# Layer 0's gate and up products by Strassen's seven products, with the down weights' Hadamard products inside the units

## The chip, the cores and the metric

The kernel runs on one core of a Trainium2 chip. The metric is the device time of one execution in microseconds (us); shown is the median of several executions. A core has TensorE (PE: matrix products into the eight banks of PSUM), VectorE (DVE), ScalarE (ACT), GpSimd (POOL, which does not read PSUM) and SyncE (SP, which issues transfers). Each engine works its own list of instructions in order; semaphores are the only order between engines.

## The reference

Two transformer layers over 2048 tokens of width 512. The part that is changed is the feed-forward block of layer 0. Its activations are 2048 wide, and a fast Walsh-Hadamard transform stands between the product of gate and up and the down projection:

```python
def fwht(x): ...                      # orthogonal, along the last axis, n = 2048
up_gate = jnp.einsum('bsd,hd->bsh', x, W1)      # (tokens 2048, 512) x (512, 2048)
up_lin  = jnp.einsum('bsd,hd->bsh', x, W3)
hidden  = jax.nn.silu(up_gate) * up_lin
hidden  = fwht(hidden)
out     = jnp.einsum('bsh,dh->bsd', hidden, W2)  # 2048 -> 512
...
h = _layernorm(x) * (1 + cb) + sb
x = x + gb * _L0_ffn_ref(h, W1, W2, W3)
```

The transform is symmetric, so the kernel applies it to the down weights W2 instead of to the activations. Layer 1 has linear attention (`_L1_attn_ref`) and then a feed-forward block of width 1408 without the transform.

## The kernel before, in words

Precision: each f32 factor is split into a high part (a cast to fp32r) and a low part (what is left), and a product of two such factors is three matmuls into one bank: high by high, low by high, high by low. That is `product`, lines 219 to 233, so all these matmuls have the lines 227, 228 and 229 whatever they compute; the names of their operands tell them apart.

Stages of one execution: modulation vectors and the projections of layer 0 (to some 206 us), softmax attention (to 776 us), output projection with the norm behind it (to 830 us), feed-forward of layer 0 (to 1375 us), layer 1's projections with linear attention (to 1530 us), its output projection and norm (to 1611 us), and its feed-forward block (to the end).

Layer 0's block is `feed_forward` (line 445). It takes the hidden width in segments of two chunks of 128, and for each segment goes over four blocks of 512 tokens. A step (one segment, one block) has two units, one for each chunk: a gate and an up product of 4 x 3 matmuls each (`up`). The down product of a step (`down_`, 4 tiles of 2 x 3 matmuls) comes one step later on PE, and DVE adds each tile to the residual `x` (`add_x`, line 736). Per unit ACT takes the Silu of the gate bank (line 678) and casts the hidden chunk's high part (661); DVE multiplies (763) and makes the low part (725). The Hadamard transform of the down weights is in two parts. GpSimd makes the part across the 16 chunks during attention and stores it as `w2_mixed`; the part inside a chunk is a product on PE with a 128 x 128 Hadamard matrix, `mix` (lines 559 and 560, two matmuls a chunk, 16 chunks, each once). The normed tokens stand ready as high and low parts for all 2048 tokens (`h2_hi`, `h2_lo`), and GpSimd has nothing to do in this block after the first weights.

Layer 1's block is `winograd_forward` (line 792). There gate and up of one chunk for a pair of 512-token blocks are a 2 x 2 product of blocks (gate and up rows by halves of the 512 inputs, against token halves), made by seven products instead of eight. A *unit* is one chunk and one half (1024) of the tokens; all chunks of the first half come first, then all of the second. A product is 2 x 3 matmuls. The seven left factors are sums of weight blocks: GpSimd makes four sums (`weight_sums_gpsimd`, lines 954 to 959), ACT casts the high parts in four pieces (`weight_hi_scalar`, 1010) and GpSimd makes the low parts (`weight_lo_gpsimd`, 1015). The seven right factors are made once for each half of the tokens, from four token sums (lines 967 to 978; for the first half on DVE, for the second on GpSimd in units 3 to 6), ACT casts (1038) and DVE low parts (1042). What comes out of the seven products is put together by ACT (`snapshot_scalar`, line 1101, product 0) and seven additions on DVE (1165 to 1196); then come Silu (1107), the product of gate and up (1205), the high part (1120) and low part (1213), for each of the two blocks. Products go round five banks, (7u + j) % 5.

The down product follows by segments, q, of two chunks (one chunk in a few segments of layer 1, whose width has 11 chunks). While the units of segment q are computed, PE makes the 8 tiles of segment q-1: in each unit one behind product 3, two behind product 4, one behind product 5 (`place_of`, line 892). Three banks serve them in turn, and a tile waits until the tile three before it has been added. The down weights of segment q are loaded, multiplied by the gate row on GpSimd (`down_gate_gpsimd`, 985, in the segment's first unit, behind the weight work of that unit, line 999), cast on ACT (1127) and made low on DVE (`down_lo`, 1229, behind the second and third tile's additions).

The order in which each engine does this is written out by hand in `Stage.tensor`, `Stage.scalar`, `Stage.vector` and `Stage.gpsimd`, and nothing else plans it. `projection_and_norm` (line 379) leads the output projection of layer 0 into `feed_forward`; `projection_and_pairs` (line 1283) does it in layer 1, and it also makes there the right factors of the first token half (`operand_hi_scalar`, `operand_lo_vector`, `token_sum_vector`). At the end of layer 0's block `linear_projections` (line 1374) hooks in its first norm: statistics, standard deviation, transposes.

In the prediction *first unit* and *second unit* of a segment are its chunks c = 0 and c = 1.

## Time and profile before

| | |
|---|---|
| median of 3 executions | 1983.14 us (1980.57 to 1985.82) |
| the profiled execution's own time | 1980.84 us |
| its span in the trace | 1978.6 us |
| PE busy | 1897.5 us, 96% |
| DVE, ACT, POOL busy | 1170.3, 707.6, 759.0 us |
| mean granted TensorE clock | 0.991 of full speed |

The profile page gives the busy time of each engine, the span in 40 slices, and the groups of instructions that cost most. PE's busy share is the sum of overlapping matmuls' recorded times, each ending later than the next begins; so 100% says that PE never stood still, and the distance of two starts is what a matmul costs. The trace can also be asked for windows of time, for the instructions of one engine in order, and for who waited for whom.

### The profile page before, as it was taken

How to read it: one execution, taken by the hardware profiler on the slowest of the kernel's cores; microseconds unless marked ns; L12 is line 12 of the kernel's file. 1: busy time of each engine (PE TensorE's matmuls, PEld its weight loads, DVE VectorE, ACT ScalarE, POOL GpSimd, SP SyncE). 2: the span in 40 equal slices, each digit the busy share in tenths (PEclk: the TensorE clock that was granted, in tenths of full speed). 3: DMA queues.
4: the chain of work that ended last, by engine and by line, in shares of the span. 5: the costliest groups of instructions: out<-in, count | busy, mean ns of one | idle time of the engine just before them, and what ended most of it. 6: DMA issues, size and time to landing. Idle time of an engine off the chain costs nothing. (4 is left out here: it accounts for less than half of the span.)

```text
span 1978.6 us, 26382 instructions
## 1 busy us (share of the span) xinstructions
PE 1897.5 (96%) x9936; PEld 1360.3 (69%) x9936; DVE 1170.3 (59%) x1956; ACT 707.6 (36%) x1275; POOL 759.0 (38%) x722
## 2 busy tenths in 40 slices
PE   7999999999999999899999999999999889998999
PEld 5677555555545545688888888887887567787877
DVE  5466877676666742853434343444432797778776
ACT  4221355555546565421111111113321234334332
POOL 1122678788776589300000000001000615656563
PEclk9999999999999999999999999999999999999999
DMA  9753422322321203110000000002000111111211
GB/s 325 267 152 113 98 55 56 87 54 56 87 44 34 60 12 107 59 43 32 32 2 33 32 23 10 0 20 70 11 6 0 33 32 49 54 54 43 89 57 53
DMA packets 80783, 120.83 MB, mean 61 GB/s; under 512 B 7008, under 2 KB 38768, under 8 KB 80624
## 3 DMA queue, kind: packets, MB, share of 16 engines
q1 hardware_dynamic: 73200, 93.96, 16.6%
q0 software_dynamic: 7456, 25.18, 4.2%
q8 instruction: 79, 1.29, 0.3%
q14 instruction: 48, 0.39, 0.1%
HBM read 93.68 MB, written 25.44 MB: 60 GB/s over the span
## 5 line engine op out<-in xcount | busy, mean ns | idle before, releaser
L1831 DVE TENSOR_REDUCE part_max<-banks 128x1 f32<-128x512 f32 (+2 forms) x640 | 356.9, 614 | 149.1 <-PE banks L1803 90.9
L2356 ACT ACTIVATE probs<-banks 128x512 f32<-128x512 f32 (+3 forms) x640 | 311.1, 538 | 268.7 <-PE banks L2271 133.3
L1803 PE MATMUL banks<-kst,qst 96*128 96x512 f32 (+2 forms) x640 | 261.3, 417 | 12.1 <-DVE part_max L1831 9.6
L2267 PE MATMUL banks<-qst,kst 98*128 98x512 f32 (+2 forms) x640 | 251.2, 412 | 0.7 <-ACT probs L2356 0.7
L1465 POOL TENSOR_TENSOR w_lo<-early_weights,w_hi 128x512 fp32r<-128x512 f32 x4 | 5.1, 1310 | 544.1 <-ACT w_hi L1439 544.1
L763 DVE TENSOR_TENSOR tokens_b<-banks,tokens_b 128x512 f32<-128x512 f32 x64 | 44.3, 692 | 251.7 <-ACT tokens_b L678 251.7
L2217 POOL TENSOR_TENSOR early_weights<-probs 128x512 f32<-128x512 f32 (+2 forms) x152 | 160.5, 1085 | 56.6 <-ACT probs L2356 56.1
L2217 POOL TENSOR_TENSOR pairs_own<-probs 128x512 f32<-128x512 f32 (+2 forms) x152 | 157.2, 1063 | 63.7 <-ACT probs L2356 63.4
L678 ACT ACTIVATE tokens_b<-banks 128x512 f32<-128x512 f32 x64 | 38.3, 598 | 395.6 <-PE banks L229 395.6
L2267 PEld LDWEIGHTS banks<-qst,kst 98*128 98x128 f32 x640 | 123.6, 194 | 64.3 <-issue 49.0
L1803 PEld LDWEIGHTS banks<-kst,qst 96*128 96x128 f32 x640 | 123.5, 193 | 59.9 <-DVE part_max L1831 47.1
L2308 PE MATMUL banks<-probs,tokens_a 128*32 128x512 f32 (+3 forms) x1280 | 140.6, 541 | 0.6 <-DVE tokens_b L2386 0.6
L227 PE MATMUL banks<-w_b_hi,w_a_hi 128*128 128x512 f32 x308 | 123.2, 400 | 16.4 <-DVE w_b_lo L1042 7.1
L228 PE MATMUL banks<-w_b_lo,w_a_hi 128*128 128x512 f32 x308 | 120.8, 392 | 0.0
L229 PE MATMUL banks<-w_b_hi,w_a_lo 128*128 128x512 f32 x308 | 120.7, 392 | 0.0
L736 DVE TENSOR_TENSOR tokens_a<-banks,tokens_a 128x512 f32<-128x512 f32 x128 | 86.8, 688 | 46.2 <-PE banks L229 46.2
L227 PE MATMUL banks<-f_d_hi,f_hid_hi 128*128 128x512 f32 x256 | 101.4, 396 | 1.3 <-DVE tokens_a L736 1.3
L228 PE MATMUL banks<-f_d_lo,f_hid_hi 128*128 128x512 f32 x256 | 100.1, 391 | 0.0
L229 PE MATMUL banks<-f_d_hi,f_hid_lo 128*128 128x512 f32 x256 | 100.1, 391 | 0.0
L227 PE MATMUL banks<-h_hi,f_w_first 128*128 128x512 f32 x256 | 99.7, 389 | 0.0
L228 PE MATMUL banks<-h_lo,f_w_first 128*128 128x512 f32 x256 | 99.6, 389 | 0.0
L229 PE MATMUL banks<-h_hi,f_w_first 128*128 128x512 f32 x256 | 99.6, 389 | 0.0
(263 smaller groups left out, 4188.1 us busy)
## 6 DMA issues: line engine op xcount, KB each, us to landing
tokens_a<-in_L_wmod SPq DMA_DIRECT2D x12, 1024.0 KB, 7.3
qst<-q_hi SPq DMA_DIRECT2D x32, 256.0 KB, 6.1
kst<-k_hi SPq DMA_DIRECT2D x32, 256.0 KB, 8.2
tokens_b<-in_down_wt SPq DMA_DIRECT2D x10, 512.0 KB, 3.5
q_hi<-qk_out_hi POOLq DMA_DIRECT2D x16, 256.0 KB, 3.5
q_lo<-qk_out_lo POOLq DMA_DIRECT2D x16, 256.0 KB, 3.4
k_hi<-qk_out_hi POOLq DMA_DIRECT2D x16, 256.0 KB, 3.8
k_lo<-qk_out_lo POOLq DMA_DIRECT2D x16, 256.0 KB, 4.2
```

Of the source, the lines that this page charges most:

```text
L227: nc.tensor.matmul(dst, lh, rh, start=(first and i == 0), stop=False)
L228: nc.tensor.matmul(dst, lh, rl, start=False, stop=False)
L229: mm = nc.tensor.matmul(dst, ll, rh, start=False, stop=(last and i == n - 1))
L678: nc.scalar.activation(silu[:, u % 2, :], bank[2 * (u % 2)][:], ACT.Silu, scale=1.0 if mixed else gs[:, ch:ch + 1]).then_inc(silu_s, 1)
L736: nc.vector.tensor_tensor(xt, bank[4 + n % 3][:], xt, ALU.add).then_inc(x_added, 1)
L763: nc.vector.tensor_tensor(act_[:, u % 2, :], up_bank, silu[:, u % 2, :], ALU.mult).then_inc(hid_s, 1)
L1803: mm = nc.tensor.matmul(dst[:, 0:wide], qst[n % QS][0:BIASROW, h, P * t:P * t + P], kst[(NB * g + c) % KS][0:BIASROW, h, 0:wide], start=Tr ...
L1831: nc.vector.tensor_reduce(part_max[:, n % 2, ht, c:c + 1], max_bank(slot)[:, 0:wide], AX_X, ALU.max).then_inc(max_read, 1)
L2217: nc.gpsimd.tensor_tensor(pairs[o % 2][:, h, c0:512], probs[:, 2 * s % PS, h, c0:512], probs[:, (2 * s + 1) % PS, h, c0:512], ALU.add).the ...
L2267: mm = nc.tensor.matmul(dst[:, c0:512], kst[ck % KS][0:BIASROW + 2, h, at:at + P], qst[n % QS][0:BIASROW + 2, h, c0:512], start=True, stop ...
L2308: mm = nc.tensor.matmul(bank[6][HD * h:HD * h + HD, c0:512], v[:, kt, at:at + HD], probs[:, q % PS, h, c0:512], start=(kt == 0), stop=(las ...
L2356: nc.scalar.activation(probs[:, q % PS, h, c0:512], score_bank(sh)[:, c0:512], ACT.Exp, scale=SCALE).then_inc(exp_done, 1)
```

## The change

`feed_forward` and `projection_and_norm` are deleted. Layer 0's block is now made by `winograd_forward`, which takes a mode `mixed` for the case without scales and with Hadamard weights. With 16 chunks it has 32 units and 16 segments of two chunks each. What differs in this mode from layer 1's:

- The Hadamard products of segment q stand in its second unit: that of chunk 0 behind product 0, that of chunk 1 behind product 4 (`mixes`). For segment 0 they stand in unit 2, the first unit of segment 1. They are made for each token half anew, 32 instead of 16. Both use bank 7, so the down tiles have two banks instead of three.
- Down weights pass ACT and DVE twice: split before the Hadamard product (`down_hi`, `down_lo`, counted by `m_hi_s`, `m_ready`) and again out of bank 7 (`mixed_hi`, `mixed_lo`, counted by `d_hi_s`, `d_ready`).
- In unit 2 all four down tiles stand behind product 5.
- Gate and up are multiplied in place (`made`), with no scale of the unit's rows.
- The norm behind the block is hooked into units 27 (statistics, DVE), 28 (standard deviation, ACT) and 29 (normalization, DVE), and its transposes and low parts between the last eight down tiles.

Both layers get: one semaphore for all products, one for what DVE has taken and so on (their order is each engine's own, so that no wait changes its meaning); the gating of segment 0's down weights on GpSimd one unit later (in unit 1, behind the weights of unit 2); and the second half of the last block's transposes behind product 5 of unit 1 instead of product 3.

```diff
 (winograd_forward)
+            mixed = down_s is None
+            DOWN_BANKS = 2 if mixed else 3
-            SEG_AT = [0, 2, 4] + list(range(5, NCH + 1, 2))
+            SEG_AT = [0, 2, 4] + list(range(5 if NCH % 2 else 6, NCH + 1, 2))
...
+            def mixed_segment(u):
+                q, c = segment(u)
+                if not mixed or u < 2:
+                    return None
+                return 0 if u == 2 else q if c else None
+
+            def mixes(u, j):
+                q = mixed_segment(u)
+                return [] if q is None or j not in (0, 4) else [(q, j // 4)]
...
             def place_of(u):
+                if mixed and u == 2:
+                    return ([], [], tiles)
...
                 def gpsimd(pool):
-                    Stage.weight_sums_gpsimd(pool, 0)
                     for u in range(UNITS):
...
-                        if c == 0:
+                        if c == (q == 0):
                             Stage.down_gate_gpsimd(pool, q)
...
 (Stage.tensor)
+                        if n >= DOWN_BANKS:
+                            pe.wait_ge(x_added, n - DOWN_BANKS + 1)
...
+                    def mix(q, c):
+                        n = 2 * q + c
+                        pe.wait_ge(m_ready, n + 1)
+                        if n == 0:
+                            pe.wait_ge(norm.h_ready, KT * NB)
+                        else:
+                            pe.wait_ge(d_ready, n)
+                        nc.tensor.matmul(bank[7][:], hadamard[:], dh[:, q % 2, c, :], start=True, stop=False)
+                        nc.tensor.matmul(bank[7][:], hadamard[:], dl[:, q % 2, c, :], start=False, stop=True).then_inc(mix_mm, 1)
...
-                            if u == 1 and j in (0, 3):
-                                turn(NB - 1, j // 3)
+                            if u == 1 and j == 0:
+                                turn(NB - 1, 0)
...
-                        gate_up(u, 5)
+                        gate_up_and_mix(u, 5)
+                        if u == 1:
+                            turn(NB - 1, 1)
...
                     for t in range(8):
+                        if behind and t % 4 == 0:
+                            behind.first_tensor(pe, t // 4)
                         down_(2 * SEGS - 1, t)
 (Stage.scalar)
                             Stage.snapshot_scalar(act, u)
+                            if mixed_segment(u) is not None:
+                                mixed_hi(mixed_segment(u), 0)
                             hidden_hi(u - 1, 1)
                             Stage.weight_hi_scalar(act, u, 3)
...
                         if c == (q == 0):
                             down_hi(q)
+                        if mixed_segment(u) is not None:
+                            mixed_hi(mixed_segment(u), 1)
                         hidden_hi(u, 0)
+                        if behind and u == UNITS - 4:
+                            behind.ahead_scalar(act)
 (Stage.vector)
                         add_trunk2(u)
+                        if mixed_segment(u) is not None:
+                            mixed_lo(mixed_segment(u), 0)
                         add_gate1_part(u)
...
                             down_lo(q)
                         add_up0(u)
-                        hidden(u, 0)
+                        if mixed_segment(u) is not None:
+                            mixed_lo(mixed_segment(u), 1)
+                        make_hidden(u, 0)
                         for q, t in last:
                             add_x(q, t)
                         hidden_lo(u, 0)
+                        if behind and u == UNITS - 5:
+                            behind.ahead_statistics_vector(dve)
+                        if behind and u == UNITS - 3:
+                            behind.ahead_z_vector(dve)
...
+                    def mixed_lo(q, c):
+                        dve.wait_ge(d_hi_s, 2 * q + c + 1)
+                        nc.vector.tensor_tensor(dl[:, q % 2, c, :], bank[7][:], dh[:, q % 2, c, :],
+                                                ALU.subtract).then_inc(d_ready, 1)
...
-            forward = feed_forward(ctx, alloc, alloc("f0_w_first", [P, 4 * KT * 2 * P], F32R), "f0_", 0, FFN0,
-                                   a["w1t"], a["w3t"], w2_mixed, H0, out_p, norm2, next_w=a["w_qkv1"][0])
+            forward = winograd_forward(alloc, lambda name: sem(ctx, name), "f0_", 0, a["w1t"], a["w3t"], w2_mixed, H0, out_p, norm2,
+                                       ctx0, lambda i: tokens_b[:, 2048 * i:2048 * i + 1024], "v_", next_w=a["w_qkv1"][0])
...
-            on_tensor, on_scalar, on_vector = projection_and_norm(out_p, norm2, forward, prepared=2, behind=linear)
+            on_tensor, on_scalar, on_vector = projection_and_pairs(out_p, norm2, forward, ctx0, nothing, nothing,
+                                                                   lambda act: None, prepared=2, behind=linear)
```

## Rows read from the trace of the kernel before

**Rows 1.** Windows of stages: window, its length, busy (instructions) by engine, PE's clock, DMA.
```profile
900.00:1300.00 400.00, 400.00 (x1762) 329.88 (x1761) 166.03 (x246) 70.83 (x114) 0.00 (x0) 1.00 0.06 20
...
1815.10:1844.95 29.85, 29.85 (x133) 24.75 (x132) 22.11 (x32) 11.31 (x22) 17.74 (x18) 1.00 0.15 45
...
1780.00:1810.00 30.00, 24.77 (x98) 18.53 (x97) 27.51 (x32) 15.66 (x24) 22.95 (x18) 0.94 0.12 36
1615.00:1645.00 30.00, 21.39 (x94) 16.51 (x94) 23.83 (x36) 16.69 (x27) 16.46 (x17) 0.94 0.19 53
```
**Rows 2.** PE in order, inside layer 1's block: start, length, line, operands.
```profile
1699.72 0.39 PE L228 MATMUL banks<-w_b_lo,w_a_hi 128*128 128x512 f32 x1
...
1712.87 0.39 PE L229 MATMUL banks<-w_b_hi,w_a_lo 128*128 128x512 f32 x1
```
**Rows 3.** Groups of instructions, 829 to 1376 us: one of nine alike of layer 0.
```profile
L228 PE MATMUL banks<-h_lo,f_w_first 128*128 128x512 f32 x256 | 99.6, 389 | 0.0
```
**Rows 4.** PE in order, layer 0: last transposes before its block, and its end.
```profile
829.77 1.09 PE L183 MATMUL banks<-ident,n_z 128*128 128x128 f32 x8 [0.78 <-DVE n_z L163]
...
1374.78 0.50 PE L227 MATMUL banks<-ht_hi,w_hi 128*128 128x512 f32 x1 [0.81 <-DVE v_tile L1575]
```
**Rows 5.** ACT in order, units 13 and 14 of layer 1.
```profile
1815.10 0.57 ACT L1101 COPY w_sums<-banks 128x512 f32<-128x512 f32 x1
...
1828.71 0.62 ACT L1010 CAST w_a_hi<-tokens_b 128x512 fp32r<-128x512 f32 x1
...
1844.93 0.57 ACT L1101 COPY w_sums<-banks 128x512 f32<-128x512 f32 x1
```
**Rows 6.** GpSimd in order, unit 13 of layer 1.
```profile
1829.41 1.30 POOL L1015 TENSOR_TENSOR w_a_lo<-tokens_b,w_a_hi 128x512 fp32r<-128x512 f32 x1 [4.17 <-ACT w_a_hi L1010]
...
1833.70 3.25 POOL L1015 TENSOR_TENSOR w_a_lo<-early_weights,w_a_hi 128x512 fp32r<-128x512 f32 x3
1836.90 2.56 POOL L985 TENSOR_TENSOR tokens_b<-tokens_b,w_drow 128x512 f32<-128x512 f32 x2
```
**Rows 7.** DVE in order, units 12 and 13 of layer 1.
```profile
1817.28 0.69 DVE L1170 TENSOR_TENSOR w_sums<-banks,w_sums 128x512 f32<-128x512 f32 x1
1818.06 0.69 DVE L1177 TENSOR_TENSOR w_sums<-banks,w_sums 128x512 f32<-128x512 f32 x1
...
1838.89 1.95 DVE L1229 TENSOR_TENSOR w_d_lo<-tokens_b,w_d_hi 128x512 fp32r<-128x512 f32 x2 [2.06 <-ACT w_d_hi L1127]
1840.76 0.68 DVE L1191 TENSOR_TENSOR w_sums<-banks,w_sums 128x512 f32<-128x512 f32 x1
```
**Rows 8.** PE in order, units 0 and 1 of layer 1.
```profile
1627.90 0.47 PE L227 MATMUL banks<-w_b_hi,w_a_hi 128*128 128x512 f32 x1 [1.58 <-POOL w_a_lo L1015]
...
1639.22 1.83 PE L183 MATMUL banks<-ident,n_z 128*128 128x128 f32 x8 [3.99 <-ACT tokens_b L1288]
```
**Rows 9.** ACT in order, unit 1 of layer 1, behind those transposes.
```profile
1640.23 1.63 ACT L1288 ACTIVATE tokens_b<-banks,mod_cols 128x512 f32<-128x512 f32 x2 [0.49 <-PE banks L183]
1641.76 1.12 ACT L1010 CAST w_a_hi<-early_weights 128x512 fp32r<-128x512 f32 x2
```
**Rows 10.** DVE and ACT in order, last norm before layer 0's block.
```profile
823.75 2.47 DVE L137 BATCH_NORM_STATS2 n_stats<-tokens_a 128x6 f32<-128x512 f32 x4
...
827.80 1.92 DVE L163 TENSOR_SCALAR n_z<-tokens_a,n_mv,n_rstd 128x512 f32<-128x512 f32 x4
...
839.46 1.28 ACT L678 ACT_TABLE_LOAD   x1
```
**Rows 11.** DVE and GpSimd in order, unit 5 of layer 1, side by side.
```profile
1710.95 3.89 DVE L1229 TENSOR_TENSOR w_d_lo<-tokens_b,w_d_hi 128x512 fp32r<-128x512 f32 x2 [3.88 <-ACT w_d_hi L1127]
...
1711.46 2.83 POOL L973 TENSOR_TENSOR tokens_b<-tokens_b 128x1024 f32<-128x1024 f32 x1
```
**Rows 12.** DVE in order, last units of layer 1's first token half.
```profile
1784.41 1.26 DVE L1042 TENSOR_TENSOR w_b_lo<-tokens_b,w_b_hi 128x1024 fp32r<-128x1024 f32 x1
```

More of the change, by code:

```diff
@@ L205, in h_scalar, with split_vector @@
                             hi(k)
-            def split_vector(self, dve, b):
-                for k in range(KT):
+            def split_vector(self, dve, b, chunks=range(KT)):
+                for k in chunks:
                     i = KT * b + k
@@ L304, in weights_vector, with bias_gpsimd @@
                     nc.vector.tensor_tensor(bias_row[:], bias_row[:], gate, ALU.mult).then_inc(bias_gated, 1)
-                def bias_gpsimd(pool):
+                def bias_gpsimd(pool, tiles=range(T)):
                     pool.wait_ge(bias_gated, 1)
-                    for t in range(T):
+                    for t in tiles:
                         res_ready(pool, t)
@@ L792, in winograd_forward @@
-        def winograd_forward(alloc, sem_, tag, layer, gate_w, up_w, down_w, hidden, out_p, norm, rows_t, spare,
-                             gate_s, up_s, down_s, store):
+        def winograd_forward(alloc, sem_, tag, layer, gate_w, up_w, down_w, hidden, out_p, norm, rows_t, spare, pre,
+                             gate_s=None, up_s=None, down_s=None, store=None, next_w=None):
             NCH = hidden // P
             UNITS = 2 * NCH
+            mixed = down_s is None
+            DOWN_BANKS = 2 if mixed else 3
@@ L1221, in add_x @@
                         xt = x[:, 8 * (q // SEGS) + t, :]
-                        nc.vector.tensor_tensor(xt, bank[5 + n % 3][:], xt, ALU.add).then_inc(x_added, 1)
+                        nc.vector.tensor_tensor(xt, down_bank(n)[:], xt, ALU.add).then_inc(x_added, 1)
                     def down_lo(q):
@@ L1276, in vector, with projection_and_pairs @@
                         add_x(2 * SEGS - 1, t)
+                        if behind and t % 4 == 3:
+                            behind.first_vector(dve, t // 4)
                 def scales_vector(dve):
-                    dve.wait_ge(scales_loaded, 64)
-                    nc.vector.tensor_tensor(drow[:], drow[:], gate[:], ALU.mult).then_inc(drow_ready, 1)
+                    if mixed:
+                        dve.wait_ge(scales_loaded, 16)
+                        nc.vector.tensor_scalar(drow[:], drow[:], float(hidden) ** -0.5, None, ALU.mult).then_inc(drow_ready, 1)
+                    else:
+                        dve.wait_ge(scales_loaded, 64)
+                        nc.vector.tensor_tensor(drow[:], drow[:], gate[:], ALU.mult).then_inc(drow_ready, 1)
             return Stage
-        def projection_and_pairs(out_p, norm, ffn, rows_t, more_tensor, more_vector, used):
+        def projection_and_pairs(out_p, norm, ffn, rows_t, more_tensor, more_vector, used, prepared=1, behind=None):
             def rows_scalar(act, b):
@@ L1298, in tensor @@
                         norm.tensor(pe, b - 1)
-                ffn.tensor(pe, lambda b, half: norm.tensor(pe, b, first=2 * half, end=2 * half + 2))
+                ffn.tensor(pe, lambda b, half: norm.tensor(pe, b, first=2 * half, end=2 * half + 2), behind)
             def scalar(act):
-                out_p.hi_scalar(act, 1)
+                if prepared > 1:
+                    act.wait_ge(out_p.parts_ready, prepared)
+                else:
+                    out_p.hi_scalar(act, 1)
                 for b in range(NB):
@@ L1370, in vector @@
                 ffn.operand_lo_vector(dve, 0, 5)
-                ffn.vector(dve, lambda: norm.z_vector(dve, NB - 1))
+                ffn.vector(dve, lambda: norm.z_vector(dve, NB - 1), behind)
             return tensor, scalar, vector
@@ L1452, in sync @@
                     load_decay(sp, 0)
-                    sp.wait_ge(before.upped, before.units)
+                    sp.wait_ge(before.products_done, before.all_products)
                     for i in range(1, 3):
```

660 lines of the change are left out of this document (171 added, 489 removed).

## The prediction

> **What bounds the kernel now.** I read the windows first. From 900 to 1300 us, inside layer 0's block, PE is busy 400.00 of 400 us, DVE 166.03, ACT 70.83 and GpSimd 0.00 [rows 1]: only PE's work and PE's own waits count there. What a matmul costs is not its recorded 389 ns but the distance of two starts: 58 steps from 1699.72 to 1712.87 us [rows 2] are 0.2267 us each. Then I asked what layer 1's block costs, since it already runs the scheme that layer 0 gets. In units 13 and 14 PE never stands, with DVE busy 22.11 of 29.85 us; but from 1780 to 1810, where the token half changes, and from 1615 to 1645, where the block starts, PE has 98 and 94 matmuls in 30 us [rows 1]. So the scheme is PE-bound in its middle and late at its joints. The chain of work at a joint decides.
>
> **The work that goes.** Layer 0's block has nine groups of 256 matmuls [rows 3] and 32 Hadamard matmuls, 2336. After: 32 units x 7 x 6 = 1344, down tiles 128 x 6 = 768, Hadamard 64, together 2176. The 160 that go are 36.3 us. Of the block's 545.0 us (829.8 to 1374.8 [rows 4]), 2336 x 0.2267 = 529.6 are matmuls, some 7.4 transposes (six groups of eight, 1.09 us and more [rows 4]), and 8.0 waiting. This waiting is replaced by what follows.
>
> The Trainium skill ("TensorE: Matmul & The Clock Gate", Back-to-back issue gap) gives about 131 ns for a 512-column matmul in a stream of weight loads and matmuls. By that the 160 would be worth 21 us and the total below would be 15 us later; the trace says 226.7 ns, and I use that.
>
> **The start of the block (+28.3 us of PE idle).** I walk the four lists. Up to the projection's end they do what they did, with DVE's two low parts of old tokens replaced by token sums and right factors of 1.1 to 1.2 us each [rows 12]; the projection ends at about 828.6, 1.2 us earlier. Block 2's transposes then wait for DVE's norm (2.3 us), product 5 for its right factor (1.8), unit 1 for its weights behind the Silu table load (1.9; layer 1 shows 1.58 [rows 8], the load 1.28 [rows 10]), with 0.5 more for a bank: 6.7 idle so far, unit 1 starts at T = 847.0. Now comes a chain, as delays from T:
> - products 0 to 5 and eight transposes, the last eight transposes begin at 9.9; ACT has the last rows at +2.5 (layer 1: 1639.22 to 1641.76 [rows 8, 9]), 12.4, and the first weight cast of unit 2 at 12.95;
> - GpSimd: three low parts of unit 2 (3.2 [rows 6]), then the moved gating of segment 0 (2.56 [rows 6]), 18.8; cast and low part of chunk 1, 20.1;
> - DVE and ACT: the addition of product 5, product of gate and up, high and low part, the addition of product 6, Silu, unit 2's snapshot, the new cast, high part: 26.0, where ACT casts the last weights of unit 2;
> - in a first unit the down weights' low parts begin 10.2 us after that cast (1828.71 to 1838.89 [rows 5, 7]) and end at 12.1. In unit 2 the low part out of bank 7 for chunk 1 stands behind them and behind product 5's addition, so the first down tile can't start before 26.0 + 13.4 = 39.4. PE's own work would bring it there at about 21.
> - four tiles and product 6: unit 3 starts at 46.3, against 27.6 by PE's work alone.
> So 18.7 more, 1.0 for GpSimd stretching the norm beside it, 1.7 for the clock: the granted clock means 0.94 in the window with layer 1's start, where it lay at 1.2 of 2.4 GHz for a part of the time after PE stood [rows 1]. Bounds: 20 (chain overlapped by a third) to 33.
>
> **The middle (+3.9).** Two units have 132 matmuls plus 4, 30.8 us; DVE gets two operations more, of 0.69 us, ACT two of 0.6. None is on PE's path as such. But the Hadamard product behind product 4 waits until the first one's result has been read by DVE. Snapshot start to the end of the third addition's predecessor is 2.96 us (1815.10 to 1818.06 [rows 5, 7]); 0.2 for the cast put between and 0.69 for the low part make 3.85. The snapshot comes 4.9 us after PE started the unit (PE's starts counted back from the end of product 3), so bank 7 is free at 8.75, and PE is there at 8.61. It is the tightest wait of the scheme: whatever makes a second unit's snapshot later is a stall of PE of that size. Those 0.14, and a half of the 0.5 that two more DVE operations of 0.61 to 0.69 us add to the way to the next snapshot (the other half I give to a Silu without a row of scales), make about 0.3 us a segment; in 13 segments 3.9. Bounds 0 and 14. Two banks for the down tiles instead of three cost nothing here: the third tile of a unit starts 2.7 us after the first ended, and DVE adds it within 0.7 to 1.4. Second halves' token sums on GpSimd in units 3 to 6 stretch the down weights' low parts: 3.89 us beside one of them against 1.95 without [rows 7, 11]. Two meet them: +2.0 (0 to 4).
>
> **The change of token half (+9.5).** In layer 1 98 matmuls instead of 132 in the window [rows 1] are 7.8 us; units 15 and 16 have DVE there at 27.51 of 30 us, and two operations more make 1.4, the casts 0.3. Bounds 8 and 13.
>
> **The norm hooked in (+6.5).** Before, it hid in DVE's free time. Now it stands in a list with no slack: statistics in unit 27 are 3.0 us (2.47 and the rest [rows 10]), a table load back to Silu in unit 28 adds 1.4, normalization in unit 29 2.1 (1.92 and a reciprocal [rows 10]). By the tight wait each reaches PE. Bounds 2 and 9.
>
> **The end (+2.2).** Eight tiles on two banks: DVE comes to them after the last low part, 4.7 us after product 6, so the third tile stands 1.65; 0.5 for the first weights of the next stage. Bounds 0 and 4.
>
> **Layer 1 (+2.5).** The 3.99 us wait of the moved transposes [rows 8] shrinks, since products 4 and 5 run ahead of them: -2.7. But the moved gating puts segment 0's down weights, and product 5's addition behind them, some 4 us later in unit 1, which stops product 3 of unit 2 (+2.4 net of the gain) and again that of unit 3 (+1.5), less what the clock gives back (1.4). Bounds -2 and +5. Attention, layer 0's projections and linear attention are untouched. New transfers are as layer 1's, small, and SP's list puts none of them in front of one that is due.
>
> **Sum** against the profiled execution's own 1980.8 us: -36.3 + 28.3 + 3.9 + 2.0 + 9.5 + 6.5 + 2.2 + 2.5 - 8.0 - 1.2 = +9.4, so 1990.2. The median lies 2.3 above that execution: 1992.5.
>
> **Rivals.**
> *A, PE-bound but for layer 1's joints.* The start costs what layer 1's does: 94 of 132 matmuls, with 16 transposes worth 3 us in the window, are some 6 us, doubled for the projection's share 12; the hooked norm stays hidden. Then -36.3 + 12 + 9.5 + 2 - 8 - 1 = -22, 1961. For it: a middle with DVE idle 7.7 of 29.85 us [rows 1]. Against it: the order of unit 2, where the down tiles' weights stand behind the next segment's.
> *B, DVE becomes the bound.* GpSimd was idle and will work 17.7 of 30 us beside DVE. The place is DVE's list in each second unit: where beside GpSimd an operation on two SBUF tiles takes twice its time, as the down weights' low parts did [rows 11], the result of the first Hadamard product leaves bank 7 later by as much. One more microsecond each in 15 segments, and in the joints, is +20: 2012. It decides from 0.3 us more per segment on, the slack being none. Against it: rows of layer 1's middle already contain GpSimd's work, and PE does not stand in them.
> The Trainium skill ("GPSIMD Engine Reference", Specifications) says that GpSimd's SBUF interfaces are shared with VectorE, with contention where a DVE instruction has two SBUF inputs; it speaks for B, and at the low parts of [rows 11] the trace agrees (3.89 against 1.95 us).
> *C, the start's chain is shorter by half*, with the rest as forecast: +9.4 - 10 = -1, 1982.
>
> **How the numbers follow.** From no change a measurement of this kernel can tell some 0.3%, 6 us (1977 to 1989). Forecast 1992 (own range 1982 to 2003) 0.50, of which 0.12 lies under 1989; C 0.15, nearly all of it within 0.3%; A 0.18, all faster; B 0.17. Faster 0.19, same 0.26, slower 0.55. The range leaves out half of A and a part of B: 1966 to 2010.
>
> **What would show it.** Layer 0's block has 2176 matmuls, and 0.2267 us between them where PE works. PE stands in unit 2 in front of its first down tile for about 10 us, released by DVE's low part out of bank 7; in front of Hadamard products for tenths of a microsecond in most second units, and for 2 to 5 in units 29 and 31; some 9 us where the token half changes. In layer 1 the wait of 3.99 us gives way to waits in units 2 and 3. The forecast is wrong if the block takes less than 530 us or more than 565, if unit 2's first tile waits under 5 us, or if PE in the middle of the block stands more than 1 us a segment.

## The result, and the profile after

| | before | after |
|---|---|---|
| median (5 executions each) | 1981.87 us | 1991.78 us (1990.86 to 1992.32) |
| ratio after to before | | 1.0047, 95% interval 1.0032 to 1.0061 |
| span of the profiled execution | 1978.6 us | 1990.4 us |
| mean granted TensorE clock | 0.991 | 0.983 |

The change makes the kernel slower by 0.5%. The forecast was 1992. First the page of the kernel after: busy times, and the groups of the new block.

```profile
PE 1878.7 (94%) x9776; PEld 1336.4 (67%) x9776; DVE 1331.9 (67%) x2180; ACT 807.8 (41%) x1467; POOL 1042.1 (52%) x1002
...
L227 PE MATMUL banks<-v_b_hi,v_a_hi 128*128 128x512 f32 x448 | 176.9, 395 | 10.4 <-DVE v_b_lo L682 6.7
L899 DVE TENSOR_TENSOR tokens_a<-banks,tokens_a 128x512 f32<-128x512 f32 x224 | 152.2, 686 | 49.5 <-PE banks L229 48.2
```

PE was busy 1897.5 us and is now 1878.7; DVE went from 1170.3 to 1331.9, GpSimd from 759.0 to 1042.1. The 448 matmuls of each of the three kinds are 32 units x 7 x 2: with 768 down and 64 Hadamard matmuls the 2176 of the forecast. So the work went, and the time did not. The windows of the block (busy us of PE, PEld, DVE, ACT, POOL, each with its count of instructions; granted clock; DMA share; GB/s) say where, beside those of before [rows 1]:

```profile
829.00:860.00 31.00, 24.62 (x114) 18.57 (x113) 28.67 (x51) 13.77 (x22) 8.90 (x10) 0.99 0.17 51
860.00:900.00 40.00, 26.71 (x94) 20.84 (x93) 17.77 (x26) 12.01 (x22) 17.07 (x18) 0.79 0.17 53
900.00:1000.00 100.00, 95.79 (x413) 77.83 (x412) 72.81 (x100) 34.62 (x65) 62.66 (x58) 0.98 0.14 43
1000.00:1100.00 100.00, 100.00 (x443) 82.81 (x442) 73.98 (x113) 41.10 (x76) 54.44 (x57) 1.00 0.17 53
1100.00:1130.00 30.00, 25.38 (x108) 19.50 (x107) 27.30 (x33) 12.95 (x21) 20.35 (x16) 1.00 0.14 37
1130.00:1290.00 160.00, 160.00 (x708) 132.44 (x707) 118.13 (x179) 63.06 (x118) 88.53 (x92) 1.00 0.17 53
```

From 1130 to 1290 PE makes 708 matmuls in 160 us, 0.226 each: the middle is PE-bound without a gap, with DVE at 74%. The loss is in the start (94 matmuls in 40 us at a clock of 0.79) and at the change of token half (108 in 30). PE's own timeline names each wait. Columns: start, duration, engine, line, operation, operands; in brackets the idle time before it and who ended it.

```profile
819.74 1.32 PE L183 MATMUL banks<-ident,n_z 128*128 128x128 f32 x8 [2.47 <-ACT tokens_b L984]
...
844.01 0.47 PE L227 MATMUL banks<-v_b_hi,v_a_hi 128*128 128x512 f32 x1 [2.12 <-DVE v_b_lo L682]
...
851.43 0.50 PE L227 MATMUL banks<-v_b_hi,v_a_hi 128*128 128x512 f32 x1 [0.23 <-DVE v_sums L861]
...
859.02 0.47 PE L227 MATMUL banks<-v_b_hi,v_a_hi 128*128 128x512 f32 x1 [1.85 <-POOL v_a_lo L655]
...
865.94 0.47 PE L227 MATMUL banks<-v_b_hi,v_a_hi 128*128 128x512 f32 x1 [1.45 <-POOL v_a_lo L655]
...
870.77 0.80 PE L727 MATMUL banks<-v_d_hi,hadamard 128*128 128x512 f32 x1 [3.20 <-DVE v_d_lo L906]
...
890.14 0.79 PE L227 MATMUL banks<-v_d_hi,v_hid_hi 128*128 128x512 f32 x1 [8.63 <-DVE v_d_lo L911]
...
939.65 0.47 PE L727 MATMUL banks<-v_d_hi,hadamard 128*128 128x512 f32 x1 [1.32 <-DVE v_d_lo L911]
...
974.19 0.47 PE L727 MATMUL banks<-v_d_hi,hadamard 128*128 128x512 f32 x1 [2.52 <-DVE v_d_lo L911]
...
1113.57 0.47 PE L227 MATMUL banks<-v_b_hi,v_a_hi 128*128 128x512 f32 x1 [1.52 <-DVE v_b_lo L682]
...
1324.75 0.47 PE L727 MATMUL banks<-v_d_hi,hadamard 128*128 128x512 f32 x1 [2.28 <-DVE v_d_lo L911]
...
1381.29 0.50 PE L227 MATMUL banks<-ht_hi,w_hi 128*128 128x512 f32 x1 [3.09 <-DVE v_tile L1280]
```

The 8.63 us is the wait that the forecast put at 9.6, and its releaser is the forecast one, the low part out of bank 7. Between 974.19 and 1110, and from 1123 to 1314, no row has a wait. Two lines of that middle, DVE's and PE's, show how near it is:

```profile
1196.39 0.68 DVE L911 TENSOR_TENSOR v_d_lo<-banks,v_d_hi 128x512 fp32r<-128x512 f32 x1
```

```profile
1197.72 0.39 PE L727 MATMUL banks<-v_d_hi,hadamard 128*128 128x512 f32 x1
```

Bank 7 is read until 1197.07, and PE is there at 1197.72. Here is the chain in front of 890.14, one fence for each engine (GpSimd, ScalarE, VectorE):

```profile
867.68 2.48 POOL L626 TENSOR_TENSOR tokens_b<-tokens_b,early_gate 128x512 f32<-128x512 f32 x2
...
885.03 2.48 POOL L626 TENSOR_TENSOR tokens_b<-tokens_b,early_gate 128x512 f32<-128x512 f32 x2
```

```profile
887.55 0.62 ACT L789 CAST v_d_hi<-tokens_b 128x512 fp32r<-128x512 f32 x1 [0.60 <-POOL tokens_b L626]
888.07 0.58 ACT L793 CAST v_d_hi<-banks 128x512 fp32r<-128x512 f32 x1
```

```profile
869.70 1.85 DVE L906 TENSOR_TENSOR v_d_lo<-tokens_b,v_d_hi 128x512 fp32r<-128x512 f32 x2 [9.07 <-ACT v_d_hi L789]
...
886.98 1.92 DVE L906 TENSOR_TENSOR v_d_lo<-tokens_b,v_d_hi 128x512 fp32r<-128x512 f32 x2 [5.83 <-ACT v_d_hi L789]
888.81 0.68 DVE L866 TENSOR_TENSOR v_sums<-banks,v_sums 128x512 f32<-128x512 f32 x1
889.41 0.68 DVE L911 TENSOR_TENSOR v_d_lo<-banks,v_d_hi 128x512 fp32r<-128x512 f32 x1
```

L793 and L911 are segment 0's second Hadamard product, done at 880; ScalarE and VectorE come to it only behind L789 and L906, segment 1's down weights, which GpSimd gates from 885.03 on. VectorE stood 5.83 us in front.

**What a wait costs.** The idle time in brackets is too short, since PE's recorded time runs on after the moment at which the next matmul could have started (0.39 us recorded against 0.23 between starts), and since the first matmul behind a stop takes 0.31 us to the next start (865.94 to 866.25). In a kernel below with one more stall of 0.53 us in every segment, the distance of two segments' Hadamard products is 31.63 us; 136 matmuls of 0.2267 us are 30.83. A stall is therefore worth its idle time and some 0.27 us.

In layer 1 the wait of 3.99 us [rows 8] has given way to others, from 1639.44 on:

```profile
1639.44 0.50 PE L227 MATMUL banks<-w_b_hi,w_a_hi 128*128 128x512 f32 x1 [0.23 <-DVE w_sums L861]
...
1647.24 0.47 PE L227 MATMUL banks<-w_b_hi,w_a_hi 128*128 128x512 f32 x1 [2.04 <-POOL w_a_lo L655]
...
1654.00 0.47 PE L227 MATMUL banks<-w_b_hi,w_a_hi 128*128 128x512 f32 x1 [1.25 <-POOL w_a_lo L655]
...
1660.32 0.50 PE L227 MATMUL banks<-w_b_hi,w_a_hi 128*128 128x512 f32 x1 [1.96 <-DVE w_sums L866]
...
1914.98 0.47 PE L227 MATMUL banks<-w_b_hi,w_a_hi 128*128 128x512 f32 x1 [0.62 <-POOL w_a_lo L655]
```

### The profile page after: what moved, and what is told of

Same layout as the page of the kernel before. It is cut to its first block and busy times, and to the rows that moved or that the text cites. A ratio compares the mean times of both kernels' runs of the same rounds, so it can differ in the third digit from the quotient of the medians.

```text
span 1990.4 us, 27331 instructions
## 1 busy us (share of the span) xinstructions
PE 1878.7 (94%) x9776; PEld 1336.4 (67%) x9776; DVE 1331.9 (67%) x2180; ACT 807.8 (41%) x1467; POOL 1042.1 (52%) x1002
## 3 DMA queue, kind: packets, MB, share of 16 engines
q8 instruction: 78, 1.28, 0.3%
## 5 line engine op out<-in xcount | busy, mean ns | idle before, releaser
L227 PE MATMUL banks<-v_b_hi,v_a_hi 128*128 128x512 f32 x448 | 176.9, 395 | 10.4 <-DVE v_b_lo L682 6.7
L899 DVE TENSOR_TENSOR tokens_a<-banks,tokens_a 128x512 f32<-128x512 f32 x224 | 152.2, 686 | 49.5 <-PE banks L229 48.2
L229 PE MATMUL banks<-v_b_hi,v_a_lo 128*128 128x512 f32 x448 | 175.7, 392 | 0.0
L228 PE MATMUL banks<-v_b_lo,v_a_hi 128*128 128x512 f32 x448 | 175.6, 392 | 0.0
L655 POOL TENSOR_TENSOR v_a_lo<-tokens_b,v_a_hi 128x512 fp32r<-128x512 f32 (+1 forms) x60 | 69.1, 1175 | 119.9 <-ACT v_a_hi L650 119.9
L655 POOL TENSOR_TENSOR v_a_lo<-early_weights,v_a_hi 128x512 fp32r<-128x512 f32 (+1 forms) x60 | 71.0, 1207 | 95.3 <-ACT v_a_hi L650 95.3
L227 PE MATMUL banks<-v_d_hi,v_hid_hi 128*128 128x512 f32 x256 | 101.5, 396 | 9.2 <-DVE v_d_lo L911 8.6
L227 PEld LDWEIGHTS banks<-v_b_hi,v_a_hi 128*128 128x128 f32 x448 | 85.1, 190 | 32.0 <-issue 13.7
L228 PE MATMUL banks<-v_d_lo,v_hid_hi 128*128 128x512 f32 x256 | 101.1, 395 | 0.0
L229 PE MATMUL banks<-v_d_hi,v_hid_lo 128*128 128x512 f32 x256 | 100.7, 394 | 0.0
```

Source lines behind the costliest of these rows:

```text
L227: nc.tensor.matmul(dst, lh, rh, start=(first and i == 0), stop=False)
L228: nc.tensor.matmul(dst, lh, rl, start=False, stop=False)
L229: mm = nc.tensor.matmul(dst, ll, rh, start=False, stop=(last and i == n - 1))
L655: nc.gpsimd.tensor_tensor(a_lo[:, lo:hi, :, :], raw(u, lo, hi), a_hi[:, lo:hi, :, :], ALU.subtract).then_inc(a_ready, 1)
L899: nc.vector.tensor_tensor(xt, down_bank(n)[:], xt, ALU.add).then_inc(x_added, 1)
```

## The experiments

Medians of these kernels scatter by 2 to 5 us, much of it ahead of anything that the experiments touch: the output projection starts between 770.1 and 780.2 us in their traces. So each is also read between two instructions that both traces have: *mark A* is the product behind block 3's first transposes (851.43 after), *B* the Hadamard product that waits in unit 5 (939.65), *C* the one in unit 7 (974.19). A to B takes 88.22 us after, and 88.19 to 88.24 in the four kernels below that touch nothing there (1, 4, 6 and 8). Over longer stretches a stretch at the lower clock, which some traces have behind a stop and others don't, can add 1.3 to 1.7 us.

**1. Layer 1's two moves undone.**

```diff
-                        if c == (q == 0):
+                        if c == (mixed and q == 0):
                             Stage.down_gate_gpsimd(pool, q)
-                            if u == 1 and j == 0:
-                                turn(NB - 1, 0)
+                            if u == 1 and (j == 0 or j == 3 and not mixed):
+                                turn(NB - 1, j // 3)
...
-                        if u == 1:
+                        if u == 1 and mixed:
                             turn(NB - 1, 1)
```

> Layer 1's block alone gets back its two old places: segment 0's down weights are gated in unit 0, and the last transposes stand behind product 3 of unit 1. Theory 1 (the two moves cost layer 1 what its part of the trace grew by, 609.1 against 603.8 us): 5.3 us faster than the changed kernel, 1986.5. Theory 2 (the prediction's step, +2.5): 1989.3. Theory 3 (layer 1 grew for another reason, the clock it is handed or the renumbered semaphores): no change, 1991.8.

Measured: 1989.77 us, ratio to before 1.0036 (1.0023 to 1.0048). From 1639.44 to the last wait at 1914.98 layer 1 takes 275.54 us after, here 272.09, before 272.29. So the moves cost 3.3 us, and undoing them gives 3.5 back. The seven other kernels with the moves take 274.2 to 276.2 us between these two instructions, the two of the last experiment, without them, 270.8 and 271.6. Theory 2 is nearest. The other 2 us by which the rest of the trace had grown are ahead of this stretch: undoing the moves doesn't touch them.

**2. Unit 2's queues.** VectorE (shown) and ScalarE alike:

```diff
+                        late = mixed and u == 2
-                        if c == (q == 0):
+                        if c == (q == 0) and not late:
                             down_lo(q)
                         add_up0(u)
                         if mixed_segment(u) is not None:
                             mixed_lo(mixed_segment(u), 1)
...
                         hidden_lo(u, 0)
+                        if late:
+                            down_lo(1)
```

> In unit 2 of layer 0, ScalarE and VectorE take the second Hadamard product out of bank 7 ahead of splitting segment 1's down weights, which now come behind the unit's four additions. Theory 1 (the prediction's: the first down tile is late because its weights stand in the queue behind GpSimd's gating for the next segment): the wait of 8.63 us falls under 1 us, about 8 us faster than the changed kernel, 1984. Theory 2 (the chain through unit 2 is late as a whole, and the next segment's down weights are then late for the first Hadamard product of unit 3): half is given back there, 1988. Theory 3 (rival C's sense, something else in the start sets the time): 1991.

Measured: 1985.84 us, 1.0017 (1.0007 to 1.0027). A to B: 80.78 us against 88.22, so 7.4 us. The wait did not fall under 1 us; PE's row:

```profile
882.12 0.50 PE L227 MATMUL banks<-v_d_hi,v_hid_hi 128*128 128x512 f32 x1 [2.95 <-DVE v_d_lo L914]
```

The gain is nearly what theory 1 said: between A and B PE waits 11.5 us in place of 16.4, and most of the other 2.5 us is matmuls and transposes that no longer run at the lower clock behind the long stop. The cause of the largest wait is shown: the order of two queues, not the amount of work. This one edit takes the kernel from 1.0047 to 1.0017.

**3. Segment 0's gating in unit 0 of layer 0.**

```diff
-                        if c == (q == 0):
+                        if c == (q == 0 and not mixed):
                             Stage.down_gate_gpsimd(pool, q)
```

> Segment 0's down weights of layer 0 are gated on GpSimd in unit 0 again, as layer 1 had it before the change; layer 1 stays as changed. GpSimd stands from 848.7 to 857 us in the changed kernel, and its gating stands from 867.7 on, with VectorE idle 9 us behind it. Theory 1 (the moved gating is the head of unit 2's chain): the wait in front of the first Hadamard product, 3.20 us, goes, and all of the chain behind it comes 3 us earlier: 3 to 3.5 us faster than the changed kernel, 1988.5. Theory 2 (the chain through unit 2 hangs on segment 1's down weights, which are gated only at 885): the wait only moves to the first down tile, no change, 1991.8.

Measured: 1990.85 us, 1.0042 (1.0028 to 1.0056). A to B: 86.60, a gain of 1.6. The 3.20 us wait at the first Hadamard product is gone, and most of it stands again at the second, while the first down tile's shrinks from 8.63 to 7.37:

```profile
875.97 0.63 PE L727 MATMUL banks<-v_d_hi,hadamard 128*128 128x512 f32 x1 [2.48 <-DVE v_d_lo L911]
...
886.96 0.79 PE L227 MATMUL banks<-v_d_hi,v_hid_hi 128*128 128x512 f32 x1 [7.37 <-DVE v_d_lo L911]
```

Both theories in part: the moved gating costs 1.6 us alone, and the rest of its 3 us only moves to the waits behind it.

**4. The hooked norm in VectorE's gaps** (first lines VectorE, last lines ScalarE in front of the down weights' casts; the old calls are gone).

```diff
+                        if behind and u == UNITS - 6:
+                            behind.ahead_statistics_vector(dve)
+                        if behind and u == UNITS - 4:
+                            behind.ahead_z_vector(dve)
                         q, c = segment(u)
                         if c == (q == 0):
                             down_lo(q)
...
+                        if behind and u == UNITS - 5:
+                            behind.ahead_scalar(act)
+                            nc.scalar.activation(norm.ve[:, 0, :], norm.ve[:, 0, :], ACT.Silu)
```

> The norm hooked in behind layer 0's block is put where its engine stands anyway: statistics and normalization in front of the down weights' low parts of units 26 and 28 (there VectorE waits 1.8 to 4.5 us for ScalarE), the standard deviation into ScalarE's gap of unit 27, with a small Silu behind it so that the table comes back there. Theory 1 (the placing costs what PE waits in units 29 and 31, 0.99 + 2.28 + 0.19 + 0.81 us): 4.3 us faster, 1987.5. Theory 2 (the prediction's +6.5): 1985.3. Theory 3 (VectorE is full in this stretch, so that its 5 us reach PE wherever they stand): no change.

Measured: 1988.85 us, 1.0031 (1.0019 to 1.0043). From C to the waiting down tile at the end (1368.82 after): 389.67 us, against 392.94 and 392.92 in kernels 2 and 6, which have the norm where the change put it and, unlike the trace after (394.63), no stretch at the lower clock behind C. 3.3 us, theory 1 less the two waits that stay:

```profile
1308.86 0.50 PE L727 MATMUL banks<-v_d_hi,hadamard 128*128 128x512 f32 x1 [0.83 <-DVE v_d_lo L907]
...
1316.98 0.47 PE L727 MATMUL banks<-v_d_hi,hadamard 128*128 128x512 f32 x1 [0.58 <-DVE v_d_lo L912]
```

**5. The slack of bank 7.**

```diff
                         dve.wait_ge(d_hi_s, 2 * q + c + 1)
+                        if c == 0 and q:
+                            for i in range(2):
+                                dve.wait_ge(more, 2 * (q - 1))
+                                nc.vector.bn_stats(norm.stats[:, i, :], bank[7][:]).then_inc(more, 1)
                         nc.vector.tensor_tensor(dl[:, q % 2, c, :], bank[7][:], dh[:, q % 2, c, :],
...
```

> In each second unit of segments 1 to 15 of layer 0, VectorE reads bank 7 twice more (two statistics operations of about 0.6 us each, results unused) in front of the low part of the first Hadamard product. This delays by 1.2 us the moment at which bank 7 is free. Theory 1 (the trace after: bank 7 is free some 0.65 us before PE is there): 0.55 us for each of 15 segments, 8 us slower than the changed kernel, 2000. Theory 2 (the prediction's tight wait, without slack): 1.2 to 1.35 us for each, 18 to 20 us slower, 2011. Theory 3 (rival B: VectorE's list is the bound in the whole segment): 18 us too, but then PE also stands in front of gate and up products in first units. Theory 4 (the wait is far from tight): under 2 us.

Measured: 2006.52 us, 1.0121 (1.0106 to 1.0137), 14.7 us more than after. Every segment of the middle has the same wait:

```profile
1012.46 0.47 PE L728 MATMUL banks<-v_d_hi,hadamard 128*128 128x512 f32 x1 [0.53 <-DVE v_d_lo L916]
...
1044.08 0.47 PE L728 MATMUL banks<-v_d_hi,hadamard 128*128 128x512 f32 x1 [0.53 <-DVE v_d_lo L916]
```

A delay of 1.2 us costs 0.80 us a segment (31.63 against 30.83), so the slack is 0.4 us: theory 1 for the wait, with the 0.27 us on top that it had left out. Nine such segments are 7.2 us; most of the rest is at the joints, where what was late already is later by the whole delay (2.51 us at B for 1.32, 3.47 in unit 29 for 2.28). The median lies between theory 1's 2000 and theory 2's 2011. Rival B as a bound of VectorE's whole list is out: no wait stands in front of gate and up products of first units.

**6. The next weights' casts between the norm's chunks** (the loop over `w_hi` is called in `h_scalar` in front of chunk 2, and no more behind it).

> Behind layer 0's block ScalarE casts the next projection's weights between the second and the third chunk of the norm, not behind the fourth, so that GpSimd's low parts of them (5.5 us) run ahead of VectorE's last two low parts of the tokens, which took 3.51 us beside them instead of 1.28. Theory 1 (contention at the end): the wait at the end of the block, 3.1 to 4.2 us, falls under 1.5: 2 to 3 us faster, 1989.3. Theory 2 (the additions in front of them set the time): no change, or a microsecond slower, since the third chunk of the norm comes 2 us later.

Measured: 1990.75 us, 1.0045 (1.0028 to 1.0062). From unit 31's Hadamard wait to the end of the block: 23.76 us, against 25.26 to 25.32 in kernels 2, 3 and 7 (24.17 after). That is 1.5 us against those three and 0.4 against the trace after itself, under the forecast 2 to 3; the last wait is 2.01 us, not under 1.5. The contention moved: the earlier two low parts of the tokens now stand beside GpSimd's.

```profile
1366.45 2.69 DVE L216 TENSOR_TENSOR ht_lo<-tokens_b,ht_hi 128x512 fp32r<-128x512 f32 x2
...
1373.46 1.28 DVE L216 TENSOR_TENSOR ht_lo<-tokens_b,ht_hi 128x512 fp32r<-128x512 f32 x2
```

**7. The second half's token sums in units 3, 5, 7 and 9** (before: 3 to 6).

> The four token sums of the second half on GpSimd in layer 0 stand in units 3, 5, 7 and 9 in place of 3 to 6, so that none meets the down weights' low parts of a first unit. Theory 1 (the three waits of 1.32, 0.37 and 2.52 us between 939 and 975 come from VectorE's operations stretched beside the sums): 3 to 5 us faster than the changed kernel, 1988. Theory 2 (rival B: GpSimd's work beside VectorE costs the same wherever it stands): the waits move to units 7 and 9, no change.

Measured: 1991.38 us, 1.0051 (1.0034 to 1.0067). From A to the change of half 256.84 us, against 257.37 and 257.39 in kernels 4 and 6. Theory 2: the three waits became five, of 0.79, 0.36, 0.76, 0.37 and 0.80 us. The down weights' low parts are no longer stretched: they take 1.95 us in each of these units. But three of the sums (2.40 us each) now run beside VectorE's product of gate and up, and then the low parts come late. VectorE:

```profile
977.26 2.88 DVE L881 TENSOR_TENSOR v_sums<-v_sums 128x512 f32<-128x512 f32 x1
...
994.25 1.95 DVE L906 TENSOR_TENSOR v_d_lo<-tokens_b,v_d_hi 128x512 fp32r<-128x512 f32 x2 [3.90 <-ACT v_d_hi L789]
```

L881 takes 0.69 us without a sum beside it, 2.2 less. ScalarE, which waits for it, casts the next weights later, GpSimd gates the down weights later, and VectorE stands 3.90 us in front of their low parts where 1.78 is usual. These 2.1 us less the slack of 0.4 are 1.7, and the two waits that follow (0.36 and 0.76, with 0.27 each) are 1.66. So an operation stretched beside GpSimd reaches PE in either kind of unit, as long as the lists have this order; the last experiment changes it.

**8. Two right factors' low parts on GpSimd at the change of half** (`b_lo` of products 3 and 4, at the end of unit 15, with a semaphore of their own).

> At layer 0's change of token half GpSimd makes the low parts of right factors 3 and 4, at the end of unit 15, in place of VectorE. Theory 1 (VectorE's list is the bound at this joint: 27.3 of 30 us): two operations of 1.1 to 1.2 us leave it; the four waits of 0.99, 1.52, 1.47 and 0.64 us fall by half, 2.5 to 3 us faster, 1989. Theory 2 (the two engines share their way to SBUF, so that VectorE's other low parts are stretched by as much): no change. Theory 3: GpSimd takes twice VectorE's time for them and its weights for unit 16 come late: 1 to 3 us slower.

Measured: 1995.61 us, 1.0072 (1.0055 to 1.009). From C to unit 29's first Hadamard product 342.89 us, against 339.03 to 339.06 in kernels 2, 4 and 6. But 1.6 of these 3.8 us lie ahead of the edit, in a stretch at the lower clock behind C that the trace after has too; from the last matmul of unit 15 on it is 208.02 against 205.78 to 205.84 us, 2.2 slower. GpSimd and VectorE, and then PE:

```profile
1104.29 5.31 POOL L660 TENSOR_TENSOR v_a_lo<-early_weights,v_a_hi 128x512 fp32r<-128x512 f32 x3
1109.55 2.85 POOL L645 TENSOR_TENSOR v_b_lo<-v_t,v_b_hi 128x1024 fp32r<-128x1024 f32 x1
1112.36 2.79 POOL L645 TENSOR_TENSOR v_b_lo<-tokens_b,v_b_hi 128x1024 fp32r<-128x1024 f32 x1
```

```profile
1106.53 1.21 DVE L687 TENSOR_TENSOR v_b_lo<-tokens_b,v_b_hi 128x1024 fp32r<-128x1024 f32 x1
...
1110.84 2.10 DVE L897 TENSOR_TENSOR v_hid_lo<-v_sums,v_hid_hi 128x512 fp32r<-128x512 f32 x1
1112.87 3.35 DVE L687 TENSOR_TENSOR v_b_lo<-v_t,v_b_hi 128x1024 fp32r<-128x1024 f32 x1
```

```profile
1116.37 0.77 PE L227 MATMUL banks<-v_b_hi,v_a_hi 128*128 128x512 f32 x1 [4.52 <-DVE v_b_lo L687]
1116.94 0.63 PE L228 MATMUL banks<-v_b_lo,v_a_hi 128*128 128x512 f32 x1
```

The four waits (4.6 us and 0.27 for each, 5.7) became two (4.52 and 0.38, together 5.4). So the waiting did not grow; the 2.2 us are the lower clock behind the long wait, 0.77 granted from 1110 to 1125 where the trace after has 1.00. Theory 2 for the waits: VectorE's `v_b_lo` beside GpSimd's takes 3.35 us, and an operation of 512 columns 2.10 us where it takes 0.69. At 1106.53 VectorE kept its 1.21 us, and GpSimd paid: its three low parts took 5.31 us, in the steady middle 3.25. The work that was moved to GpSimd came back on one of the two. The Trainium skill ("GPSIMD Engine Reference", Specifications) says that GpSimd's SBUF interfaces are shared with VectorE, with contention where a VectorE instruction has two SBUF inputs; these rows agree, and the additions out of PSUM beside the same work keep their 0.68 us.

**9 and 10. Together.** The first (*joints1*) has edits 1 to 4, 6 and 7, gating in unit 0 in both layers, and in unit 2 on ScalarE the second Hadamard product ahead of the casts that wait for unit 3's weight sums. The second (*joints2*) adds, from segment 2 on in layer 0, the gating ahead of the weight sums, and on ScalarE the casts behind the first weight cast:

```diff
                             Stage.weight_lo_gpsimd(pool, u, 3)
+                        q, c = segment(u)
+                        first_gate = mixed and c == 0 and q >= 2
+                        if first_gate:
+                            Stage.down_gate_gpsimd(pool, q)
                         if u + 1 < UNITS:
...
                                 Stage.weight_hi_scalar(act, u + 1, i)
+                                if mixed and i == 0 and segment(u)[1] == 0 and segment(u)[0] >= 2:
+                                    down_hi(segment(u)[0])
```

> Together: layer 1's two old places, segment 0's gating in unit 0 in both layers, unit 2 with the second Hadamard product taken out first (on ScalarE now also ahead of the casts that wait for unit 3's weight sums), the hooked norm in VectorE's gaps, the next weights' casts between the norm's chunks, token sums in units 3, 5, 7, 9. Theory 1 (the stalls are separate and at the joints alone; each is worth what its own run gained between the same two instructions of its trace: 3.2, 1.6, 7.5 and some 2 more in unit 2, 3.3, 1.5, 2.2): 1991.8 - 21 = 1971, faster than the kernel before by 0.5%. Theory 2 (they overlap: behind each wait the next one stands): half of it, 1981, no change against before. Theory 3 (rival B, the extra work of VectorE and GpSimd itself): 1988.

> As joints1, and from segment 2 on layer 0's down weights are gated ahead of the weight sums on GpSimd and cast behind the first weight cast on ScalarE, so that VectorE, which stands 1.8 us in front of their low parts in each first unit, needn't. Theory 1 (in the middle PE has no wait, so the gap costs nothing; only the joints gain: the waits of 0.83 and 0.58 us that are left in unit 29 and part of the change of half): 1 to 3 us faster than joints1, 1969. Theory 2 (the gap covered GpSimd's weight work, which now comes 2.6 us later): product 0 or 2 of the second units waits, 0.5 us for each, 7 us slower than joints1.

Measured: joints1 1968.91 us, ratio to before 0.9933 (0.9921 to 0.9944); joints2 1966.45 us, 0.9924 (0.9912 to 0.9937). Both are faster than the kernel before (1983.12 us beside them) and than the change alone (22.9 us for the first, theory 1). The second's lead of 2.5 us is within the scatter of the medians, and it isn't where theory 1 looked for it: unit 29's waits stay (0.90 and 0.56 us). But with the gating first, the five waits of the token sums are gone, and PE stands nowhere from 882 to 1091, though the down weights' low parts now take 2.63 to 3.42 us in place of 1.95; VectorE no longer waits for ScalarE in front of them:

```profile
881.19 0.50 PE L229 MATMUL banks<-v_d_hi,v_hid_hi 128*128 128x512 f32 x1 [1.38 <-DVE v_d_lo L925]
...
1092.44 0.47 PE L229 MATMUL banks<-v_b_hi,v_a_hi 128*128 128x512 f32 x1 [0.58 <-DVE v_b_lo L688]
```

## Why the prediction was right, point by point

The total, the sign and the largest wait were right; the terms were right only in sum. Measured ones are from the trace after, each stall its idle time and 0.27 us.

| step | predicted | measured |
|---|---|---|
| 160 matmuls fewer | -36.3 | -36.3 (2176 are there, 0.2267 us each) |
| the projection | -1.2 | +1.7 |
| start of the block | +28.3 | +26 |
| middle, with token sums | +3.9 + 2.0 | +6.9 |
| change of token half | +9.5 | +5.7 |
| the hooked norm | +6.5 | +5.4 |
| end of the block | +2.2 | +4.2 |
| layer 1's moves | +2.5 | +3.3 |
| between the blocks; ahead of them | 0 | +2.1; +1.3 |
| old waiting, and all that isn't listed | -8.0 | -8.5 (the rest of the sum) |
| sum | +9.4 | +11.8 |

**The start** was right in place and size. Unit 1 starts at 847.17 (forecast 847.0), the first down tile at 890.14 (886.4), unit 3 at 897.37 (893.3), with 1.3 us of delay already in hand when the projection began. From the end of the moved gating (870.16) to the tile it took 20.0 us where the walk had 20.6. The part that was missing is ahead of it, inside unit 1: 1.32 us at 850.11 for the norm's rows, whose normalization took 3.88 us beside GpSimd's low parts and 1.92 without, and 1.85 us at 859.02 for a low part of GpSimd. They put the last transposes at 861.27, where the walk had 856.9, and with them the gating 4 us later. The clock cost 4.4 us there, of which I had put 1.7. Experiment 2 shows the mechanism, experiment 3 that of the gating. The forecast's own terms are added up wrongly by 0.4: the waits ahead of unit 1 are 6.5, not 6.7, and all of the start 27.9, not 28.3.

**The projection** failed as a step. I let it end earlier by the operations that DVE loses; the trace has a wait of 2.47 us for ScalarE's rows in it, at 819.74, which I had not walked.

**The middle** failed in its mechanism. The tight wait is real, but bank 7 has 0.4 us of slack and no segment without other work stalls: the snapshot comes 4.47 us after the unit's start, not 4.9, and snapshot to low part takes 3.49 us, not 3.85. What I priced at 3.9 us is 0. In its place the token sums cost 5.0 us, not 2.0 (waits of 1.32, 0.37 and 2.52 us), since by the tight wait each stretched operation comes through to PE, and nearly all of the other 1.9 us is one stretch at the lower clock behind the last of them (975.70 to 978.69, matmuls 0.43 us apart). That the two terms together come within a microsecond is luck: their errors cancel. The term was also added up too low by its own numbers, since 0.14 and a half of 0.5 are 0.39 a segment, 5.1 us and not 3.9.

**The change of half** was too dear. Layer 1's loss there was scaled up by two more operations; the four waits after are 4.6 us, and the last two as long as in layer 1 (1.47 and 0.64 us against 1.45 and 0.63). What remains is VectorE's list, at 27.3 of 30 us; experiment 8 moved two operations of it to GpSimd, and PE's waits there stayed 5.4 us.

**The norm** was right: waits at the Hadamard products behind the statistics and behind the table loads (0.99 and 2.28 us), little behind the normalization (0.81 us in unit 31, where the forecast had 2 to 5). **The end** was too cheap: contention again, 2.36 us for two low parts that take 1.28 alone. **Layer 1** was right within a microsecond: its part grew by 3.3, and undoing the moves gives 3.5.

**The rivals.** A is the nearest to what the change could give: the block's joints cost more than layer 1's because of two queue orders and three placings, and with these mended the kernel stands at 1966 to 1969, 5 to 8 us above A's 1961. B is no bound of the middle, as experiment 5 shows; as contention at single places it is in experiments 6, 7 and 8. C is what experiment 2 makes of the kernel: 1985.8 against its 1982.

What stays open: the separate gains between marks add up to 17.8 us (3.5, 7.4, 1.6, 3.3, 1.5, 0.5), and joints1 has 22.9. The 5 us between them lie in the start: the 280 matmuls from A on take 88.22 us after and 74.12 in joints1, 14.1 less, where experiments 2 and 3 gave 9.0. Of the 14.1, 9.9 are shorter waits, and most of the rest is matmuls that no longer run at the lower clock. Whether unit 2's further edit on ScalarE made the difference or the sum of the two others wasn't measured alone, and no run here holds the clock and changes the waits.

## What to carry to other kernels

A scheme that saves matmuls pays only if the chains at its joints are walked engine by engine: here more than the 36 us saved were lost, most of them in some 20 waits of 0.2 to 9 us and the lower clock behind them, and 23 to 25 us came back by reordering queues, without one operation less. Where an instruction that is due stands behind one that waits for another engine's later work, the order of the queue is the first thing to mend. A tight wait without a stall isn't free either: its slack (0.4 us here) decides what contention elsewhere costs, so measure it by adding work until PE stops. And judge a trial by the waits and the clock between two marks: of the 3.8 us by which experiment 8 seemed slower, 1.6 lay ahead of its edit.

## What the runs showed of the hardware

- An idle time in PE's timeline understates the stall by 0.27 us in this stream.
- After the long stops PE runs at the lower clock for a while: 0.79 granted from 860 to 900, with matmuls recorded at 0.63 us and 0.43 apart from 890.74 on, and 0.39 and 0.23 apart again from 893.70.
- Operations of VectorE with two SBUF inputs take two to four times as long beside GpSimd's, or GpSimd's take longer beside them: 3.35 us for 1.21, 3.51 for 1.28 in kernel 4, 2.88 for 0.69 in kernel 7, on GpSimd 5.31 for 3.25. The normalization, with one tensor and two columns out of SBUF, takes 3.88 us beside GpSimd's low parts and 1.92 without. Those of VectorE that read PSUM keep their time (0.68 us).
